# A transformer layer with a mixture of experts on one core: the layer-normed input is fed to the first product raw and by features, and its norm is applied behind the product

## The reference

```
n   = layernorm(x)                       # over the 512 features, no gain, no offset
cq  = n @ Wc  + bc                       # 128 wide
ckv = n @ Wckv + bckv                    # 128 wide
kr  = rope(n @ Wkr + bkr)                # 256 wide
q   = [cq @ Wcq + bcq, rope(cq @ Wqr + bqr)]          # 16 heads of 32 + 16
k   = [ckv @ Wck + bck, kr]
v   = ckv @ Wv + bv                      # 16 heads of 32
scores = einsum('bsid,bsjd->bsij', q, k) / sqrt(48)   # for each token, head against head: 16 x 16
out = einsum('bsij,bsjd->bsid', softmax(scores), v) @ Wo + bo
x1  = x + layernorm(out)
out = x1 + layernorm(experts(layernorm(x1)))          # 64 experts, 6 for each token, and a shared one
```

## Time and profile before

| | us |
|---|---|
| median of 3 runs (lowest, highest) | 1982.51 (1980.75, 1984.57) |
| the profiled execution, its own time | 1972.49 |
| its span, first to last instruction | 1970.5 |
| token pipeline in steady order | about 101 to 1296 of the span |
| TensorE busy in the span | 1813.3 (92%) |
| VectorE busy | 1482.7 (75%) |
| ScalarE busy | 1039.2 (53%) |
| GpSimd busy | 554.7 (28%) |
| granted TensorE clock, mean | 0.972 |

### The profile page before, as it was taken

One profiled execution on the slowest core, in us unless ns is written; L12 is line 12 of the kernel. 1 busy time (PEld: TensorE's weight loads), 2 busy tenths in 40 slices (PEclk: granted clock), 3 DMA queues, 4 the chain that ended last, 5 costly groups with the idle time before them and its releaser, 6 DMA issues. The chain is left out here.

```text
span 1970.5 us, 49884 instructions
## 1 busy us (share of the span) xinstructions
PE 1813.3 (92%) x14529; PEld 1439.2 (73%) x14529; DVE 1482.7 (75%) x3871; ACT 1039.2 (53%) x2257; POOL 554.7 (28%) x773
## 2 busy tenths in 40 slices
PE   5899999999999999999999999865799999978886
PEld 4788888888888888888888888754455555546564
DVE  6688888888888888888888888854354445439897
ACT  4666666666667676666666666631233333323333
POOL 1112111111212121212121212111344444427777
PEclk8899999999999999999999999987899999989999
DMA  5355656555555555555555555566999999979994
GB/s 194 77 155 132 157 129 158 131 148 142 140 151 141 150 138 153 136 154 136 154 136 153 137 154 133 144 155 202 307 309 312 306 308 310 291 210 398 396 397 163
DMA packets 540056, 384.01 MB, mean 195 GB/s; under 512 B 423848, under 2 KB 432168, under 8 KB 539944
## 3 DMA queue, kind: packets, MB, share of 16 engines
q1 hardware_dynamic: 519456, 324.99, 56.9%
q0 software_dynamic: 14336, 35.66, 7.9%
q10 hardware_dynamic: 6208, 22.68, 3.0%
HBM read 232.46 MB, written 150.63 MB: 194 GB/s over the span
## 5 line engine op out<-in xcount | busy, mean ns | idle before, releaser
L617 ACT COPY kT<-bank 48x256 f32<-48x256 f32 x512 | 309.0, 604 | 12.6
L895 POOL TENSOR_SCALAR ve<-mv 128x1 f32<-128x1 f32 x192 | 42.4, 221 | 959.8 <-DVE mv L728 959.8
L1103 PE MATMUL e_gu<-w,xgT 128*128 128x384 f32 x512 | 187.2, 510 | 13.9 <-issue 12.9
L617 ACT COPY qT<-bank 48x256 f32<-48x256 f32 x512 | 188.1, 367 | 13.3 <-PE bank L453 2.3
L460 PE MATMUL bank<-wgu,xfT 128*128 128x416 f32 x512 | 187.6, 366 | 4.3 <-ACT xfT L617 3.8
L461 PE MATMUL bank<-wgu,xfT 128*128 128x416 f32 x512 | 181.8, 355 | 0.0
L1264 DVE SCALAR_TENSOR_TENSOR tanh<-tanh,e_gu 128x192 f32<-128x192 f32 x64 | 22.6, 354 | 167.9 <-ACT tanh L1190 167.9
L1103 PEld LDWEIGHTS e_gu<-w,xgT 128*128 128x128 f32 x512 | 94.2, 194 | 72.4 <-issue 18.8
L1347 POOL DMA_INDIRECT acc_scratch<-eo,sidx x64 | 101.5, 1586 | 123.7 <-ACT eo L1186 107.5
L1126 PE MATMUL e_ps<-w,hidT 96*128 96x512 f32 x256 | 127.6, 621 | 1.6 <-ACT hidT L1178 0.9
L464 PE MATMUL bank<-wgu,xfT 128*128 128x416 f32 x512 | 119.2, 355 | 0.3 <-DVE xfT L737 0.3
(11 more groups left out here) (178 smaller groups left out, 4884.8 us busy)
## 6 DMA issues: line engine op xcount, KB each, us to landing
w<-w_eg SPq DMA_DIRECT2D x60, 768.0 KB, 6.0
acc_scratch<-zero SPq DMA_DIRECT2D x130, 256.0 KB, 4.1
w<-w_ed SPq DMA_DIRECT2D x60, 384.0 KB, 7.6
xf_scratch<-xf SPq DMA_DIRECT2D x64, 288.0 KB, 2.1
xin<-x SPq DMA_DIRECT2D x64, 256.0 KB, 3.0
v_scratch<-v SPq DMA_DIRECT2D x64, 256.0 KB, 3.7
vbd<-v_scratch SPq DMA_DIRECT2D x128, 128.0 KB, 3.3
o_scratch<-o SPq DMA_DIRECT2D x256, 64.0 KB, 2.3
```

Of the source, the lines that this page charges most:

```text
L617: nc.scalar.copy(dst, src).then_inc(done.sem, 1)
L1103: last = nc.tensor.matmul(gu_ps[par], xgT[:, par, n, :], w1[:, place, n, :], start=(n == 0), stop=(n == KD - 1))
```

## The change

- x is handed over a second time laid out by features (`xt`), 256 KB for each tile, and loaded to `x_raw`. The turn of `xn`, the writing of `xn` and its semaphores are gone: `xT` is copied and its low part made from `x_raw`, unnormalised.
- To take out the mean, the first product's weights are centred on the chip at the start: four products with a tile of ones (1/512) give the mean of each column in `b2`, and VectorE subtracts it from the four weight parts before they are split. The root of the variance multiplies the product's result, in the two adds, which become `scalar_tensor_tensor` with a `settle` ahead of each and in the other order (`lat` first).
- The values' products are 32 of 64 x 64 by 64 x 32, in the four parts of the array, into `b4` and `b5`; `vbd` has no zeros any more, and GpSimd's fill of it is gone. `o` is written in two operations. The first product's high part now waits for them, since it writes `b5`.
- In TensorE's order half of the probabilities are turned between the high and the low part of `wo`'s product; the turn of `lat` stands behind `wck` and goes to `b2`; the second half of k's turns stands behind the low part of the first product, and the halves have changed banks.
- In VectorE's order `chosen` stands behind the sums, the add of `wck`'s result ahead of y's statistics, and the low part of `latT` behind `o`.
- SyncE's queue issues one load more for each tile, and waits for `xT`'s low part there.

```diff
@@ start, TensorE and VectorE
+            ones = o[:, 0:P]
+            pe.wait_ge(zeroed, 2)
+            for n in range(KD):
+                pe.wait_ge(part_in[n], 16)
+                last = nc.tensor.matmul(b2, ones, parts[n][0], start=(n == 0), stop=(n == KD - 1))
+            last.then_inc(centred, 1)
+                if isinstance(i, int) and i == -1:
+                    low_x(i, par)
+                    dve.wait_ge(centred, 1)
+                    for n in range(KD):
+                        nc.vector.tensor_tensor(parts[n][0], parts[n][0], b2, ALU.subtract).then_inc(centred, 1)
@@ SyncE
+            def load_x(t, par):
+                sp.dma_start(xin[:, par, :], rows(x, t)).then_inc(x_in[par].sem, 16)
+                sp.dma_start(x_raw[:, par, :], rows(xt, t)).then_inc(x_in[par].sem, 16)
@@ TensorE
                 if active(i):
                     pe.wait_ge(a_xT.sem, a_xT.at(i))
                     pe.wait_ge(d_q.sem, d_q.at(i - 2))
+                    pe.wait_ge(d_pv.sem, d_pv.at(i - 3))
                     high(*latents)
...
-                    product(b7, [oT[:, :, n, :] for n in range(KD)], [wo[:, :, n, :] for n in range(KD)], d_oT, i - 3, pe_wo)
+                    high(*turned)
+                if active(i - 2):
+                    pe.wait_ge(a_exp.sem, a_exp.at(i - 2, 1))
+                    transposes(s0, [pr[:, n * P:(n + 1) * P] for n in range(4)], pe_pT)
+                if active(i - 3):
+                    pe.wait_ge(d_oT.sem, d_oT.at(i - 3))
+                    low(*turned, pe_wo)
...
-                if active(i + 1):
-                    pe.wait_ge(d_ln[0].sem, d_ln[0].at(i + 1))
-                    pe.wait_ge(a_kT.sem, a_kT.at(i - 2))
-                    transposes(b2, [xn[:, n * P:(n + 1) * P] for n in range(KD)], pe_xT)
...
                     for n in range(8):
-                        for g in range(2):
-                            last = nc.tensor.matmul(b4[64 * g:64 * g + 64, n * 64:n * 64 + 64],
-                                                    probT[:, n, 64 * g:64 * g + 64],
-                                                    vbd[:, par, 2 * n + g].rearrange("p b d -> p (b d)"),
-                                                    start=True, stop=True)
+                        for b in range(2):
+                            for g in range(2):
+                                h = (b + g) % 2
+                                last = nc.tensor.matmul(pv_ps[h][64 * g:64 * g + 64, n * DH:n * DH + DH],
+                                                        probT[64 * h:64 * h + 64, n, 64 * g:64 * g + 64],
+                                                        vbd[64 * h:64 * h + 64, par, 2 * n + g],
+                                                        start=True, stop=True)
@@ VectorE
+                    dve.wait_ge(g_rstd[0].sem, g_rstd[0].at(i))
+                    dve.wait_ge(pe_latT.sem, pe_latT.at(i - 1))
+                    settle(dve)
+                    scale = rstd[0][:, par:par + 1]
+                    nc.vector.scalar_tensor_tensor(lat[:], b5[:, 0:2 * DC], scale, blat[:, 0:2 * DC], ALU.mult,
+                                                   ALU.add).then_inc(d_lat.sem, 1)
                     dve.wait_ge(pe_kT.sem, pe_kT.at(i - 2))
-                    nc.vector.tensor_tensor(k[:, par, :, DH:DQ], b5[:, 2 * DC:].rearrange("p (h d) -> p h d", h=H),
...
+                    settle(dve)
+                    nc.vector.scalar_tensor_tensor(k[:, par, :, DH:DQ], b5[:, 2 * DC:].rearrange("p (h d) -> p h d", h=H),
...
-                if active(i + 1):
-                    dve.wait_ge(pe_xT.sem, pe_xT.at(i))
-                    normalise(0, xn[:], xin[:, 1 - par, :], i + 1)
...
-                    nc.vector.tensor_tensor(o[:].rearrange("p (n d) -> p n d", d=DH),
...
+                    for b in range(2):
+                        nc.vector.tensor_tensor(o[:].rearrange("p (n b d) -> p b n d", b=2, d=DH)[:, b],
...
```

More of the change, by code:

```diff
@@ L214, in token_pipeline @@
         ve = [sb(f"ve{n}", [P, 1]) for n in range(3)]
-        rstd = [sb(f"rstd{n}", [P, 1]) for n in range(3)]
+        rstd = [sb(f"rstd{n}", [P, 1 if n else 2]) for n in range(3)]
         smax4 = sb("smax4", [P, NBLK, B4])
@@ L257, in token_pipeline @@
         cast_done = sem("cast_done")
-        x_in = [count(f"x_in{n}", 16, 2, n) for n in range(2)]
+        x_in = [count(f"x_in{n}", 32, 2, n) for n in range(2)]
+        centred = sem("centred")
         xres_in = count("xres_in", 16)
@@ L298, in token_pipeline @@
         a_rank = count("a_rank")
-        d_ln = [count(f"d_ln{n}", 3) for n in range(3)]
+        d_ln = [count(f"d_ln{n}", 3 if n else 2) for n in range(3)]
         d_xT = count("d_xT")
@@ L345, in _ @@
         def _(sp):
-            for t in range(2):
-                sp.dma_start(xin[:, t, :], rows(x, t)).then_inc(x_in[t].sem, 16)
+            def load_x(t, par):
+                sp.dma_start(xin[:, par, :], rows(x, t)).then_inc(x_in[par].sem, 16)
+                sp.dma_start(x_raw[:, par, :], rows(xt, t)).then_inc(x_in[par].sem, 16)
+            load_x(0, 0)
             sp.dma_start(c[:], cst).then_inc(consts_in, 16)
@@ L387, in iteration @@
                     settle(sp)
-                    sp.dma_start(xin[:, par, :], rows(x, i + 2)).then_inc(x_in[par].sem, 16)
+                    sp.wait_ge(d_xT.sem, d_xT.at(i))
+                    settle(sp)
+                    load_x(i + 2, par)
                 if isinstance(i, int) and i == FIRST:
@@ L530, in iteration @@
                     low(*latents, pe_lat)
+                if active(i - 2):
+                    pe.wait_ge(a_qT.sem, a_qT.at(i - 2, 4))
+                    turn(k[:, par], pe_kT, 1, b3)
                 if active(i - 1):
@@ L561, in iteration @@
                     product(b4[:, 0:GU], normed, [wgu[:, :, n, GU:] for n in range(KD)], d_xfT, i - 5, pe_gu)
+                turned = b7, [oT[:, :, n, :] for n in range(KD)], [wo[:, :, n, :] for n in range(KD)]
+                pr = prob[:].rearrange("p n t h -> p (n t h)")
                 if active(i - 3):
@@ L580, in iteration @@
                     product(b6, [latT[:, 1 - par, :, 1, :]], [wck[:, :, 0, :]], d_latT, i - 1, pe_k)
-                if active(i + 1):
-                    pe.wait_ge(d_ln[0].sem, d_ln[0].at(i + 1))
-                    pe.wait_ge(a_kT.sem, a_kT.at(i - 2))
-                    transposes(b2, [xn[:, n * P:(n + 1) * P] for n in range(KD)], pe_xT)
+                if active(i):
+                    pe.wait_ge(d_lat.sem, d_lat.at(i))
+                    pe.wait_ge(a_kT.sem, a_kT.at(i - 2, 4))
+                    transposes(b2, [lat[:, n * P:(n + 1) * P] for n in range(2)], pe_latT)
                 if active(i - 5):
@@ L889, in _, with root @@
             pool.wait_ge(zeroed, 2)
-            def root(n, t):
+            def root(n, t, to):
                 pool.wait_ge(d_ln[n].sem, d_ln[n].at(t, 2))
```

125 lines of the change are left out of this document (62 added, 63 removed).

## The result

The changed kernel takes 1966.66 us (median of 17 runs, 1959.18 to 1980.26), the kernel before 1983.60 in as many (1972.02 to 1996.69). The ratio is 0.9920, with a 95% interval of 0.9902 to 0.9937: faster by 0.8%. The profiled execution took 1969.8 us, with a span of 1967.8 and a mean granted clock of 0.971.

The account below looks back on a forecast made before the run. The ring through ScalarE's `kT` was taken to bind before, VectorE's after: 19.57 against 19.89 us, -19 over 60 periods, +3 at the start, -2 in filling, together -18 from 1982.5: 1964.5 us, range 1955 to 1973.

Parts of the forecast that it names:

- start and filling: Ahead of the steady tiles: centring the first weights costs +3 us, four filling tiles lose 0.5 each, -2.
- VectorE's ring: Maxima through VectorE to `lat`, then TensorE to the next maxima: binds after the change, 19.71 and 19.25 alternating, mean 19.48 us.
- The two adds: VectorE's adds of the first product's result: they keep their length, the same per element.
- The settles: Waits ahead of each of VectorE's first-product adds: 0 if the queue runs ahead, 0.2 if not; 0.07 us taken.
- the filled gaps: On VectorE, `chosen` and the add of `wck` fill two small gaps between dependent operations: -0.1 us together.
- The turn of `xn`: On TensorE, inside the ring through ScalarE's `kT` copies: removing this step gives back 0.53 us.
- the broken product: On TensorE, turning half of the probabilities inside `wo` breaks its product in two: +0.10 us.
- The values: TensorE's 64 smaller products in four array parts: 0.1 to 0.2 us saved from 1.08.
- ScalarE's ring: Scores, TensorE to the turn of `xf`, ScalarE's copies to `kT`, scores: falls to 19.44 and 19.23, mean 19.34 us.
- the rival: The values' products cost 34 ns each, lengthening the ring through `kT` to 20.56 us: 2024 us in total, chance 0.16.
- The rival of a ring with `o` in it: First product's high part waits for `o` on VectorE: a third ring of 19.4 us; no separate chance given.
- Transfers and port: Extra load hidden, late `oin` chance 0.06; SBUF port contention between VectorE and GpSimd taken as 0, up to 1.05 us.

Follow-up runs that it names:

- the last kernel: Changed kernel with the values' products in their old form and the statistics of x moved behind the normalising of x1: 1955.92 us, ratio 0.9893 to the kernel before.

## Why the prediction came out right

Predicted were 1964.5 us and -18; measured were 1966.7 and -16.9. Most steps of the binding ring held, one ring was mis-sized and hid behind it. That the two numbers lie within 2 us of each other is in part luck: 60 periods gave -15.4 where -19 was predicted, and start and filling, predicted at +1 together, are +5.7 in the profiles. The profiled execution was to go to 1954.5 and took 1969.8; only the medians bear the forecast out.

**The bound, and where it went: right.** Before, shortening ScalarE gained 0.32 and shortening VectorE next to nothing in the regular periods. TensorE's own order, 19.35 in B, is a bound that the prediction did not price. The change takes work off it as well; by the predicted 0.43 it would be 18.92 (an estimate), below the other rings. After, the waits for `kT` are gone and those of `wq` for VectorE have taken their place.

**VectorE's ring: right in size.** 19.71 was predicted for A and 19.70 measured; 19.25 was predicted for B, where VectorE's part is 14.92 to the end of its last add (734.12), then 0.06, 3.10 and 1.22: 19.30. (TensorE's 3.10 is 3.01 in A, so up to 0.09 of it is not VectorE's.) From maxima to the last add it is 15.39 in A, predicted 15.4. Inside, two terms that differ cancelled. `o` costs 0.68 of the order (708.52 to 709.20) instead of 0.60, as predicted. The two adds don't keep their length: as `scalar_tensor_tensor` they are 0.48 and 0.47 long and stand 0.40 apart, where 0.41 and 0.34 were assumed, so +0.12 for both. The settles, for which 0.07 stood with an upper end of 0.2 that no row gives, leave no gap in these rows, and the filled gaps are worth a little more than the 0.1.

**The turn of `xn`: the mis-sized term.** It was to give back all of its 0.53, less 0.10 for the broken product. It gave 0.41, and the stretch from scores to values fell by 0.27 in B and 0.31 in A instead of 0.43. No run takes the handing over of x by features back alone, so this worth is read from rows. Before the change the copies of the probabilities ended at 707.30, and the values began at 707.86:

```profile
706.22 1.08 ACT L617 COPY probT<-score_ps 128x512 f32<-128x512 f32 x2
```

After, the second copy ends at 706.58 and the values begin at 707.15. The distance is 0.56 and 0.57; with `wo` in one piece it is 0.54, with the old values 0.56 (714.80 to 715.36), in the last kernel 0.60. As a median it is 0.55 to 0.59 in all fourteen kernels, while that from `chosen` to the values goes from 0.21 to 0.42. TensorE did not show it as a wait before since the turn of `xn` filled that time to within 0.02. When the turn went, the values could not move up by more than ScalarE's copy allowed: from `chosen` to the values is 0.35 now, against 0.22 (medians 0.11 more in B and 0.12 more in A). The broken product is what lets the second copy end earlier; without it TensorE idles ahead of the values. That the copy sets the values' start is read from these rows; no run shortened the copy by itself.

**The values: mis-sized in A.** 0.1 to 0.2 less was predicted, 0.01 less came in B and 0.21 more in A. The doubt about 34 ns for each of the smaller products was settled: 1.07 for 64 is 17 ns each. The Trainium skill (TensorE: Matmul & The Clock Gate, in its part on 56 ns against 53.3) says that products never start less than about 25 ns apart; by that figure 64 would take 1.6 us (an estimate). The trace disagrees, in the values as in the scores. What no row of before showed is the 0.16 to 0.19 of idle time behind the 64 small products where the loop begins anew.

In A 0.13 of the 0.21 is left in the ring (19.68 with the new and 19.55 with the old form, both bound by `kT`), since the stretch behind the values is shorter. With +0.12 in both and +0.13 in A the 19.44 and 19.23 of the prediction become 19.69 and 19.35; measured, with the ring laid bare, are 19.69 and 19.33. The prediction's own sums left it little room, 0.27 in A and 0.02 in B. By the same sums ScalarE's ring passes VectorE's once the values take more than 1.22 us (1.08, and 19.48 less 19.34); the 1.51 named in the rival is where the whole gain would be gone. So ScalarE's ring ties with VectorE's, and `kT` and VectorE bind B together. This is most of the difference between the mean predicted, 19.57, and the mean measured, 19.64: 0.07 in 60 periods, 4 us. The single long periods are 0.11 of the mean, predicted 0.09.

**The rival of a ring with `o` in it: half right.** The high part did not wait for `o` (`o` ended at 709.28, the product began at 709.72). But a ring through the values, `o` and VectorE's adds exists, with the length of the other two, and halving the sums laid it bare.

**Transfers and port: right.** `oin` lands 0.1 later and costs nothing, the load alone costs nothing. The low part of `xT` took 0.68 from SBUF as it had from PSUM, and the division by the gate's sum 0.25 in A as before. The Trainium skill (SBUF — State Buffer, Who interferes with whom) has a VectorE instruction with two SBUF inputs contend with a GpSimd instruction that reads SBUF. The trace can't test that here, since GpSimd's root for y ends just ahead of the low part (709.46 and 709.53 in A, 729.25 and 729.26 in B), and the low part took 0.68 in all 20 tiles.

**Start and filling: the start right, for another reason.** Centring: predicted last low part at 17.6, measured 17.84; next splits from 17.6, measured 18.67, since statistics stand between. The centring's instructions of 512 columns took 0.84 each, predicted 0.92 from a row at a granted clock of 0.50; the profile gives 1.00 for these (6 to 13 us), and why they take as long as at the lower level stays open. First maxima +3.0 predicted, 3.2 measured. But leaving the centring out gives back 1.5 only, so the 3.2 is not its price. The agreement may be luck: with the centring the first maxima lie between 43.7 and 46.4, and in the five profiles of the kernel before and its variants between 41.7 and 45.0. The filling was to gain 2 and lost 2.5 in this profile. Over the fourteen kernels that stretch, from first to fourth maxima, is between 56.3 and 62.0 us and does not go with the edits, and the experts' part lies between 669 and 690. Against a scatter of this size the profiles can't tell these terms; the medians say that they come to little.

## What to carry to other kernels

When two rings lie 0.3 us apart in 20, a change that takes more than that off the longer one alone is worth the distance, and the steps that it takes off are best costed on the second ring first. Before crediting a removed step in full, look at what the step behind it is waiting for under cover of it: here ScalarE's copy, 0.56 ahead of the values and never shown as a wait. After this change three rings tied in A within 0.05 us, and shortening ScalarE's, VectorE's, or VectorE's together with the one through the values gave nothing in A; the bound is then found by laying the rings bare one after the other.

## What the runs showed of the hardware that was not expected

- 64 products of 64 x 64 by 64 x 32 took 1.07 us, and 32 of 128 x 64 by 128 x 64 took 1.08 to 1.09: four parts of the array gave no time for half of the columns, and the scores with 64 columns take as long (1.09 to 1.10). In these two forms each instruction in four parts costs 17 ns, with 32 columns as with 64.
- With the 64 small products ahead of the loop's new start, TensorE was idle for 0.16 to 0.19 us ("issue") there, with the 32 larger ones not at all.
- `scalar_tensor_tensor` with a scalar for each partition took 0.48 us for 256 elements where `tensor_tensor` took 0.41.
- The values followed the end of ScalarE's copy by 0.54 to 0.60 us in six rows of five kernels, and by 0.55 to 0.59 as a median in all fourteen; the profile calls the idle part of it "issue" and names no engine.
